# Last layer of a four-layer kernel: each indirect transfer of POOL is sent only after the one in front of it has landed

## The chip, the cores and the metric

One core of a Trainium2 chip runs the whole program. The metric is the device time in microseconds (us) of one execution. The trace is that of one profiled execution, and its times count from the start of its span.

## The reference, cut to what matters

Four layers act on 4096 tokens of 128 features. Each layer normalises x, and adds to it the output of an attention-like block and that of a feed-forward block with experts. The change touches the fourth layer only:

```
xn = _layernorm(x, axis=-1)
x = x + _L3_attn_ref(xn, ...) + _L3_ffn_ref(xn, ...)
return x

def _L3_attn_ref(x, ...):                     # gated attention, 16 batches of 256 tokens in the kernel's tiling
    xn = (x - mu) * rsqrt(var + LN_EPS) * ln_g + ln_b
    uvz = silu(einsum('bld,df->blf', xn, W_in) + b_in)
    u, v, z = (uvz[..., :E], uvz[..., E:2 * E], uvz[..., 2 * E:])
    attn = square(relu(einsum('bqs,bks->bqk', z * gamma_q + beta_q, z * gamma_k + beta_k) / seq_len))
    out = u * einsum('bqk,bke->bqe', attn, v)
    return x + einsum('ble,ed->bld', out, W_out) + b_out

def _L3_ffn_ref(x, wg, w1, b1, w2, b2):       # one expert of 8 for each token, 640 places for each expert
    combine, dispatch = _top1_gate(tokens, wg, capacity)
    dispatched = einsum('sec,sm->ecm', dispatch, tokens)
    h = relu(einsum('ecm,emf->ecf', dispatched, w1) + b1[:, None, :])
    expert_out = einsum('ecf,efm->ecm', h, w2) + b2[:, None, :]
    return einsum('sec,ecm->sm', combine, expert_out)
```

The shapes that are given here are those that the kernel works on: N = 4096 tokens are 32 tiles (NT) of 128 tokens.

## The kernel before

The last layer is `gated_and_experts`. The normalised tokens are in SBUF (`xn_tok`). Routing (L1102 to L1228, on VectorE) works out a place for each token in the buffer `disp`, which lies in HBM: expert e owns the rows from e * 640. It is then signalled with `r_placed` (L1202).

**POOL** has two loops in this layer and nothing else of weight. The scatter (L1598 to L1601) sends 32 indirect transfers, one for each tile: 128 rows of 512 bytes (64 KB) go from `xn_tok` to their places in `disp`. All of them increment the semaphore `scattered`. Then POOL waits until the results of all experts are stored in `ybuf` (semaphores `stored`), and the gather (L1604 to L1608) sends 32 indirect transfers that fetch each token's row from `ybuf` into `gau_gb`, in 8 groups of 4 tiles, each group with its own semaphore `gathered[j]`.

**SP** waits for all 32 transfers of the scatter (L1577, 512 counts), then loads the tokens of experts 0 and 1 (L1568), and later stores results (L1574), loads weights (L1563) and stores the output in 8 pieces, one for each gathered group (L1590).

**TensorE, ScalarE and VectorE** follow a written order of 64 steps, four for each of the 16 batches of the gated attention: scores (L1657), projection (L1631, L1636), values (L1668) and the projection of v (L1648), and the output projection (L1677). Into these steps the 16 chunks of expert work are woven: chunk c belongs to step c + FIRST, FIRST = 23, and its tokens are turned one step earlier, so the first expert work (`turn_tokens`, L1692) stands in step 22, ahead of that step's values. Each engine takes its instructions in this order. The last expert result is taken in step 39, at the end of the tenth batch, and the remaining six batches follow without experts while the gather is under way.

**The combining** of the gathered rows (L1910, on VectorE) is put into the same order: group j stands at this step,

```
return max(Q_GATHER + 3 * (j + 1) + 6, 4 * (GRP * (j + 1) // QT) + 1)
```

with Q_GATHER = 40, that is at steps 49, 52, 55, 58 and 61 for groups 0 to 4, and after step 63 for groups 5 to 7. It waits for 4 transfers of its group (64 counts of `gathered[j]`).

Of the kernel before, what the change touches and what calls it, by code (L numbers as in the profile page):

```python
# [1481 lines left out]
def gated_and_experts(nc, g, t, out, disp, ybuf, r):  # L1482
# [8 lines left out]
    GRP = 4  # L1491
# [4 lines left out]
    with section(nc, "gau", *ROUTE, *names, "w_in", "xs_ready", "turned", "xt_ready",  # L1496
# [44 lines left out]
        gathered = s.sems[len(ROUTE):len(ROUTE) + NGRP]  # L1541
# [15 lines left out]
        with nc.Block() as block:  # L1557

            @block.sync
            def _(sp):  # L1560
                def load_weights(e):
                    sp.wait_ge(s.y_out, 2 * e - 2)
                    sp.dma_start(ew[:, e % 2], t["f3_packed"][e]).then_inc(ew_in[e % 2], 16)  # L1563

                def load_tokens(e):
                    if e >= 2:
                        sp.wait_ge(s.e_turned, 2 * e - 2)
                    sp.dma_start(exin[:, e % 2], disp[e * CAP3:(e + 1) * CAP3, :].rearrange("(t p) d -> p t d", p=P)  # L1568
                                 ).then_inc(ex_in[e % 2], 16)

                def store_result(c):
                    n = CUTS[c % 2][1]
                    sp.wait_ge(s.y_out, c + 1)
                    sp.dma_start(ybuf[chunk_rows(c), :].rearrange("(t p) d -> p t d", p=P),  # L1574
                                 eyo[:, c % 2, 0:n]).then_inc(stored[c % 2], 16)

                sp.wait_ge(s.scattered, NT * 16)  # L1577
                load_tokens(0)
                load_tokens(1)
                for c in range(NC):  # L1580
                    if c % 2 == 1 and c // 2 + 2 < E3:
                        load_tokens(c // 2 + 2)
                    store_result(c)
                    if c % 2 == 1 and c // 2 + 2 < E3:
                        load_weights(c // 2 + 2)
                for j in range(NGRP):
                    sp.wait_ge(s.combined, (j + 1) * GRP)
                    sp.wait_ge(s.f_taken, (j + 1) * GRP // QT)
                    tiles = slice(j * GRP, (j + 1) * GRP)
                    sp.dma_start(out.rearrange("(t p) d -> p t d", p=P)[:, tiles, :],  # L1590
                                 g.x[:, tiles, :]).then_inc(s.out_done, 16)
                sp.wait_ge(s.out_done, NGRP * 16)

            @block.gpsimd
            def _(pool):
                job.gpsimd(pool)
                pool.wait_ge(s.r_placed, 1)
                for i in range(NT):  # L1598
                    pool.indirect_dma_start(disp, bass.IndirectOffsetOnAxis(ap=r.scat_i[:, 0, i:i + 1], axis=0),
                                            g.xn[:, i, :], None, bounds_check=disp.shape[0] - 1,  # L1600
                                            oob_is_err=False).then_inc(s.scattered, 16)  # L1601
                for p in range(2):
                    pool.wait_ge(stored[p], NC // 2 * 16)
                for i in range(NT):  # L1604
                    pool.indirect_dma_start(gb[:, i, :], None, ybuf,  # L1605
                                            bass.IndirectOffsetOnAxis(ap=r.rows_i[:, 0, i:i + 1], axis=0),
                                            bounds_check=ybuf.shape[0] - 1,
                                            oob_is_err=False).then_inc(gathered[i // GRP], 16)  # L1608
# [1413 lines left out]
```

## Time and profile before

| what | us |
| --- | --- |
| median of 3 runs | 1988.49 |
| lowest, highest of them | 1988.32, 2005.57 |
| span of the profiled execution | 2006.6 |
| first transfer of the scatter starts | 1749.01 |
| SP starts to load the tokens | 1791.28 |
| first expert work on TensorE | 1820.85 |
| first transfer of the gather starts | 1926.60 |
| last combining starts | 1999.82 |

No time other than the span is recorded for the profiled execution. The three runs are of other executions of the same program; two of them agree within 0.2 us and the third is near the span. In a timeline row stand the start, the duration, the engine, the line, the operation with what it writes and reads, how many like it were merged, and in brackets how long the engine was idle before it and what the profile infers as having ended that. SP is the engine that issues the plain transfers; POOLq and SPq are the instruction queues of these engines. The busy time of an indirect transfer on POOL is the making of its descriptors; the data moves afterwards.

### The profile page before, as it was taken

Reading aid. Unit: us, or ns where it says so; the run is one execution under the profiler, and the core shown is the slowest. Engines: PE = TensorE matmul, PEld = TensorE weight load, DVE = VectorE, ACT = ScalarE, POOL = GpSimd, SP = SyncE. Lnnn points to the kernel's source line nnn. Section 1 sums busy time; section 2 is a strip of 40 time slices with the busy share of each in tenths; the row PEclk is TensorE's granted clock in tenths of the full one; section 3 lists DMA queues with packets and bytes.
Section 4 is the critical chain, followed back from the end, with each engine's and each line's share of the span. In section 5 each row is a group of like instructions: output and inputs, shape, how many; then the busy total and the mean of one; then the engine's idle time right before and its main releaser. Section 6 shows DMA issues by size and latency. Waiting matters only on the chain. (4 is left out here: it accounts for less than half of the span.)

```text
span 2006.6 us, 34124 instructions
## 1 busy us (share of the span) xinstructions
PE 1593.7 (79%) x12145; PEld 1087.2 (54%) x12146; DVE 1288.1 (64%) x2309; ACT 1058.9 (53%) x1931; POOL 797.6 (40%) x809
## 2 busy tenths in 40 slices
PE   5993788888876776758889998965799999749974
PEld 5661566666654445535567765542344444638863
DVE  7525888788788888764534457758753896724334
ACT  1345787887776764434434444545454777314421
POOL 1447766565669994374212234431400000150041
PEclk9996899999998889658989999987699999569987
DMA  5211011111001110665321124314531341211311
GB/s 151 89 56 44 22 50 56 35 49 50 28 20 35 30 29 23 229 182 88 64 57 59 59 57 81 63 25 131 103 67 42 50 67 17 95 49 51 100 43 55
DMA packets 153335, 130.56 MB, mean 65 GB/s; under 512 B 18929, under 2 KB 137864, under 8 KB 152914
## 3 DMA queue, kind: packets, MB, share of 16 engines
q1 hardware_dynamic: 140554, 104.54, 21.1%
q0 software_dynamic: 12544, 23.82, 4.3%
q8 instruction: 100, 1.64, 0.4%
q14 instruction: 65, 0.53, 0.1%
q10 hardware_dynamic: 72, 0.03, 0.0%
HBM read 77.08 MB, written 52.43 MB: 65 GB/s over the span
## 5 line engine op out<-in xcount | busy, mean ns | idle before, releaser
L746 POOL TENSOR_TENSOR xn_t<-xn_t,scan_du 128x512 f32<-128x512 f32 x256 | 320.9, 1271 | 154.9 <-ACT xn_t L893 105.1
L970 DVE TENSOR_TENSOR_SCAN xn_t<-banks,xn_t 128x512 f32<-128x512 f32 x256 | 311.5, 1217 | 78.7 <-ACT banks L883 42.0
L794 PE MATMUL banks<-scan_hc,ident 128*128 128x256 f32 x1024 | 295.4, 414 | 49.1 <-DVE scan_hc L976 49.1
L2417 ACT ACTIVATE att_pr<-banks 128x768 f32<-128x768 f32 (+1 forms) x256 | 234.3, 917 | 161.9 <-PE banks L2309 76.1
L883 ACT ACTIVATE banks<-delta,scan_exp_centre,a_neg 128x255 f32<-128x255 f32 x512 | 265.0, 559 | 14.8 <-DVE xn_t L970 14.4
L794 PEld LDWEIGHTS banks<-scan_hc,ident 128*128 128x128 f32 x1024 | 193.7, 207 | 110.2 <-DVE scan_hc L976 70.1
L976 DVE TENSOR_TENSOR scan_hc<-xn_t,banks 128x512 f32<-128x512 f32 x256 | 175.8, 687 | 33.4 <-PE banks L779 14.3
L1030 POOL DMA_INDIRECT disp<-xn_tok,places x128 | 135.3, 1057 | 154.6 <-ACT att_pr L2417 44.2
L2325 PE MATMUL banks<-att_pr,att_vx 128*32 128x256 f32 (+1 forms) x2048 | 163.6, 383 | 19.0 <-issue 9.3
L2458 DVE TENSOR_REDUCE att_mb<-banks 128x6 f32<-128x768 f32 x128 | 121.1, 954 | 89.5 <-PE banks L2283 48.7
L2462 DVE TENSOR_REDUCE att_mb<-banks 128x4 f32<-128x1024 f32 x128 | 153.9, 1221 | 18.5 <-PE banks L2276 13.4
L2276 PE MATMUL banks<-att_ks,att_qs 48*128 48x256 bf16 (+1 forms) x1024 | 118.1, 281 | 45.0 <-DMA att_ks<-k_parts 31.2
L893 ACT COPY xn_t<-banks 128x512 f32<-128x512 f32 x128 | 74.5, 582 | 123.7 <-PE banks L770 92.2
L2301 PE MATMUL banks<-att_qs,att_ks 50*128 50x256 bf16 (+1 forms) x1024 | 111.0, 272 | 13.2 <-DMA att_qs<-att_mt 11.0
L1231 POOL IOTA gau_rev<- 128x8 f32 x1 | 0.1, 138 | 302.2 <-POOLq L76 302.2
L1415 POOL DMA_DIRECT2D ybuf<-att_yo x72 | 38.8, 539 | 156.7 <-DVE att_yo L1400 153.1
L1316 PE MATMUL banks<-grouped_w,att_xt 128*128 x288 | 98.4, 465 | 0.5 <-DVE att_xt L1382 0.3
L1605 POOL DMA_INDIRECT gau_gb<-ybuf,rows x32 | 32.2, 1007 | 146.0 <-DMA ybuf<-gau_eyo 136.6
L1365 ACT ACTIVATE att_a<-banks 128x352 f32<-128x352 f32 x72 | 33.4, 463 | 104.8 <-PE banks L1316 104.8
L2276 PEld LDWEIGHTS banks<-att_ks,att_qs 48*128 48x128 bf16 x1024 | 50.1, 101 | 64.2 <-issue 28.5
L779 PE MATMUL banks<-bc,state_sel 96*128 96x256 bf16 x256 | 53.0, 290 | 34.4 <-DVE scan_hc L976 27.7
L2325 PEld LDWEIGHTS banks<-att_pr,att_vx 128*32 128x32 f32 x2048 | 43.5, 110 | 66.0 <-issue 40.7
(384 smaller groups left out, 3339.2 us busy)
## 6 DMA issues: line engine op xcount, KB each, us to landing
scan_ew<-f_packed SPq DMA_DIRECT2D x12, 578.0 KB
q_parts<-att_p_parts SPq DMA_DIRECT2D x16, 384.0 KB, 4.7
k_parts<-att_p_parts SPq DMA_DIRECT2D x16, 384.0 KB, 6.1
att_qs<-q_parts SPq DMA_DIRECT2D x64, 96.0 KB
att_ks<-k_parts SPq DMA_DIRECT2D x64, 96.0 KB
gau_ew<-f_packed SPq DMA_DIRECT2D x8, 578.0 KB
disp<-zeros SPq DMA_DIRECT2D x1, 4608.0 KB, 15.4
att_xin<-disp SPq DMA_DIRECT2D x72, 64.0 KB
```

What stands on the lines that cost most here:

```text
L746: nc.gpsimd.tensor_tensor(bu[:, i % RING], b_sb[:, q % 2], du[:, b % 2, c:c + 1, :].to_broadcast([P, 2, T]), ALU.mult).then_inc(s.bu_made, 1)
L794: ins = nc.tensor.matmul(bank(Y_BANK)[:, c, :], g.ident[:], hc[:, i % RING, n, :], start=False, stop=(i % (PAIRS * DC) == PAIRS * DC - 1 a ...
L883: ins = nc.scalar.activation(bank(DA + i % RING)[:, n, 1:T], delta[:, c, b * T + 1:(b + 1) * T], ACT.Exp, scale=a_neg[:, c, state:state + ...
L970: v.tensor_tensor_scan(rows(h[:, i % 2]), g.ps[:, DA + i % RING, :], rows(bu[:, i % RING]), 0.0, ALU.mult, ALU.add).then_inc(s.scan_done, 1)
L976: v.tensor_tensor(hc[:, i % RING], h[:, i % 2], bank(C_BANK), ALU.mult).then_inc(s.hc_ready, 1)
L1030: pool.indirect_dma_start(disp, bass.IndirectOffsetOnAxis(ap=r.scat_i[:, k, i:i + 1], axis=0), src[:, i, :], None, bounds_check=disp.shape ...
L2276: ins = nc.tensor.matmul(g.ps[:, 2 * m_slot(i) + half, lo:hi], qs[rows_of, p, j, q * P:(q + 1) * P], ks[rows_of, p, j, 0:hi - lo], start=T ...
L2301: ins = nc.tensor.matmul(g.ps[:, 2 * s_slot(i) + half, k * T:k * T + T - q0], ks[rows_of, p, j, k * P:(k + 1) * P], qs[rows_of, p, j, q0:T ...
L2325: ins = nc.tensor.matmul(g.ps[r * 32:(r + 1) * 32, O_BANK, q0:T], vx[:, b % 2, k, 4 * jg + r, :], pr[:, i % RING, half, k * T:k * T + T - q0],
L2417: nc.scalar.activation(pr[:, i % RING], g.ps[:, at:at + 2, 0:W], ACT.Exp, scale=scale).then_inc(s.p_ready, 1)
L2458: v.tensor_reduce(mb[:, b % 2, j, :].rearrange("p (g n) -> p g n", g=2), g.ps[:, at:at + 2, 0:W].rearrange("p g (n k) -> p g n k", k=P), A ...
L2462: v.tensor_reduce(mb[:, b % 2, j, :], g.ps[:, at:at + 2, :].rearrange("p g (n k) -> p (g n) k", k=T), AX_X, ALU.max).then_inc(s.m_taken, 1)
```

## The change

POOL waits ahead of each transfer but the first of each loop until the one in front of it has landed: in the scatter for i * 16 counts of `scattered`, in the gather for the counts of the group that the former transfer belongs to. Nothing else is changed: the same 64 transfers with the same data in the same order.

```
                 for i in range(NT):
+                    if i:
+                        pool.wait_ge(s.scattered, i * 16)
                     pool.indirect_dma_start(disp, bass.IndirectOffsetOnAxis(ap=r.scat_i[:, 0, i:i + 1], axis=0),
                                             g.xn[:, i, :], None, bounds_check=disp.shape[0] - 1,
                                             oob_is_err=False).then_inc(s.scattered, 16)
                 for p in range(2):
                     pool.wait_ge(stored[p], NC // 2 * 16)
                 for i in range(NT):
+                    if i:
+                        pool.wait_ge(gathered[(i - 1) // GRP], ((i - 1) % GRP + 1) * 16)
                     pool.indirect_dma_start(gb[:, i, :], None, ybuf,
                                             bass.IndirectOffsetOnAxis(ap=r.rows_i[:, 0, i:i + 1], axis=0),
                                             bounds_check=ybuf.shape[0] - 1,
```

## Rows read from the trace of the kernel before

**Rows 1.** The scatter's line in all: instructions, durations in ns, first and last start

```profile
L1599 POOLq MOVE  x32: 29/29/29, 1748.2 to 1773.4; - x32
L1599 POOL DMA_INDIRECT disp<-xn_tok,places x32: 977/977/1092, 1749.0 to 1789.1; - x32
```

**Rows 2.** Timeline of POOL, the scatter's first transfer and its last two

```profile
1749.01 1.09 POOL L1599 DMA_INDIRECT disp<-xn_tok,places  x1 [12.82 <-DVEq L1202]
...
1787.78 0.98 POOL L1599 DMA_INDIRECT disp<-xn_tok,places  x1 [0.30 <-issue]
1789.06 0.98 POOL L1599 DMA_INDIRECT disp<-xn_tok,places  x1 [0.30 <-issue]
```

**Rows 3.** Timeline of SP after the scatter, and landing of these loads

```profile
1791.28 0.95 SPq L1568 DMA_DIRECT2D gau_exin<-disp  x2
...
DMA to landing us min/median/max: 3.0/3.3/3.6
```

**Rows 4.** Timeline of TensorE from the scatter's end to the first expert work

```profile
1795.04 2.05 PE L1657 MATMUL banks<-gau_q,gau_k 128*128 128x256 f32 x4 [12.77 <-DVE x_tok L1883]
...
1802.54 1.16 PE L1677 MATMUL banks<-gau_wo,gau_gt 128*128 128x128 f32 x8
...
1804.30 1.10 PE L1657 MATMUL banks<-gau_q,gau_k 128*128 128x256 f32 x4 [0.39 <-DVE x_tok L1883]
...
1809.69 1.16 PE L1677 MATMUL banks<-gau_wo,gau_gt 128*128 128x128 f32 x8
...
1820.85 0.49 PE L1692 MATMUL banks<-ident,gau_exin 128*128 128x128 f32 x3
```

**Rows 5.** Busy time by stretch; the last three columns: TensorE's clock, DMA share, GB/s

```profile
1785.00:1791.00 6.00, 0.00 (x0) 0.00 (x0) 0.69 (x1) 0.63 (x1) 3.91 (x4) 0.50 0.13 46
1795.00:1800.00 5.00, 4.96 (x12) 4.01 (x13) 2.81 (x6) 1.45 (x5) 0.00 (x0) 0.50 0.00 0
1800.00:1810.00 10.00, 9.40 (x46) 7.38 (x45) 5.49 (x12) 3.55 (x9) 0.00 (x0) 0.99 0.00 1
1870.00:1925.00 55.00, 55.00 (x350) 47.48 (x349) 18.70 (x37) 24.24 (x52) 0.00 (x0) 1.00 0.27 80
```

**Rows 6.** The gather's line in all, and its first and last transfer on POOL

```profile
L1605 POOLq MOVE  x32: 29/29/29, 1925.8 to 1951.3; - x32
...
1926.60 1.10 POOL L1605 DMA_INDIRECT gau_gb<-ybuf,rows  x1 [136.56 <-DMA ybuf<-gau_eyo]
...
1967.27 1.00 POOL L1605 DMA_INDIRECT gau_gb<-ybuf,rows  x1 [0.31 <-issue]
```

**Rows 7.** Stretches of 0.05 us around the last data of scatter and gather

```profile
1790.60:1790.65 0.05, 0.00 (x0) 0.00 (x0) 0.00 (x0) 0.00 (x0) 0.00 (x0) 0.50 0.95 339
1790.75:1790.80 0.05, 0.00 (x0) 0.00 (x0) 0.00 (x0) 0.00 (x0) 0.00 (x0) 0.50 0.34 103
...
1969.00:1969.05 0.05, 0.00 (x0) 0.00 (x0) 0.00 (x0) 0.00 (x0) 0.00 (x0) 0.50 1.39 328
...
1969.35:1969.40 0.05, 0.00 (x0) 0.00 (x0) 0.00 (x0) 0.00 (x0) 0.00 (x0) 0.50 0.22 82
```

**Rows 8.** Timeline of VectorE in the gather and at the end, with SP's last stores

```profile
1972.09 0.69 DVE L1877 TENSOR_TENSOR gau_gt<-banks,gau_ut 128x512 f32<-128x512 f32 x1 [14.97 <-DMA k_parts<-att_p_parts]
...
1999.82 3.23 DVE L1910 SCALAR_TENSOR_TENSOR x_tok<-gau_gb,w,x_tok 128x128 f32<-128x128 f32 x12
2000.98 2.47 SPq L1590 DMA_DIRECT2D out<-x_tok  x3
```

**Rows 9.** Layer 1, a gather's transfer that waited for another engine, and its queue

```profile
L2252 POOLq MOVE  x1: 29/29/29, 1191.8 to 1191.8; - x1
...
1192.50 1.00 POOL L2252 DMA_INDIRECT att_gb<-ybuf,rows  x1 [1.53 <-PE banks L2309]
```

**Rows 10.** Layer 0, a scatter's transfer beside a long operation of VectorE

```profile
68.83 4.42 DVE L567 TENSOR_TENSOR x_tok<-x_tok,front_b_out 128x4096 f32<-128x4096 f32 x1
...
70.06 4.05 POOL L1030 DMA_INDIRECT disp<-xn_tok,places  x1 [0.30 <-issue]
```

More of the change, by code:

```diff
@@ L1598, in _ @@
                 for i in range(NT):
+                    if i:
+                        pool.wait_ge(s.scattered, i * 16)
                     pool.indirect_dma_start(disp, bass.IndirectOffsetOnAxis(ap=r.scat_i[:, 0, i:i + 1], axis=0),
@@ L1604, in _ @@
                 for i in range(NT):
+                    if i:
+                        pool.wait_ge(gathered[(i - 1) // GRP], ((i - 1) % GRP + 1) * 16)
                     pool.indirect_dma_start(gb[:, i, :], None, ybuf,
```

## The prediction

> **What bounds the kernel now.** I read the page first, then the timelines of POOL, SP, TensorE and VectorE over the last layer. The last layer has three sections in a row. In the first, POOL sends the scatter while the other engines work on the first batches of the gated attention. The scatter's 32 transfers start 1.28 us apart, from 1749.01 to 1789.06 [rows 1, 2], and SP, which waits for all of them, starts loading tokens at 1791.28 [rows 3]. That load lands about 3.3 us later, at 1794.6, and TensorE uses it at 1820.85 [rows 3, 4]. So **the scatter has 26 us of slack** and is not on the path. What sets 1820.85 is the batches. Undisturbed, one takes 7.15 us (1802.54 to 1809.69), yet TensorE was idle for 12.77 us ahead of 1795.04, for an operation of VectorE [rows 4], and VectorE worked 0.69 of 6 us from 1785 on [rows 5]. The second section, from 1820.85 to the first transfer of the gather at 1926.60, is full: TensorE is busy 55.00 of 55 us [rows 5]. It lasts 105.75 us. In the third, the gather's transfers start from 1926.60 to 1967.27 [rows 6]. Again there is a stop, 14.97 us on VectorE, ended at 1972.09 [rows 8], and the batches set the end; the last 12 combinings run without a pause from 1999.82, when their rows had long landed. So the gather isn't last now either: 1967.27 plus some 2.5 us is 30 us ahead of that.
>
> **What one paced transfer costs.** The change removes nothing, and adds 62 waits on POOL, 31 in each loop. Behind each wait stands only POOL's own next transfer; nothing else is queued there in this layer. Who waits for them is SP (scatter) and VectorE's combining (gather). The period of a paced transfer is a chain of two terms, which the back-to-back loop overlaps.
>
> (a) From the start of a transfer on POOL to the first action of an engine that waits for it. For the scatter one row has it directly: the last one starts at 1789.06 [rows 2] and SP acts at 1791.28 [rows 3], 2.22 us. It isn't delayed by a queue in front of it: its data moves in one burst from 1790.60 to about 1790.80 [rows 7], long after that of the one before (started at 1787.78). For the gather no waiter is visible. Its last transfer starts at 1967.27 [rows 6] and its data moves from 1969.00 to about 1969.35 [rows 7], 2.1 us after the start against 1.75 us in the scatter. With the scatter's 0.45 us from the end of the burst to SP's action this gives 2.55 us. Bounds: 2.1 (nothing after the burst) and 2.8.
>
> (b) From POOL's release to the start of the transfer. Now POOL's queue runs ahead (its last MOVE for the scatter is at 1773.4, the last transfer at 1789.1 [rows 1]), so this is hidden. A queue that stands at a wait can't run ahead. The row where it did stand: MOVE at 1748.2, transfer at 1749.01, 0.8 us [rows 1, 2]; in the gather 1925.8 to 1926.60, 0.8 us [rows 6]; in layer 1 1191.8 to 1192.50, 0.7 us [rows 9]. I take 0.8. Bounds: 0 (if the part after the wait still overlapped) and 0.9, since the transfers after a long pause also took 1.09 instead of 0.98 us [rows 1].
>
> So **the period is 3.02 us in the scatter** (2.22 + 0.8) and **3.35 us in the gather** (2.55 + 0.8), for 1.28 and 1.31 now.
>
> Here a rule of the Trainium skill speaks against so high a price. "DMA: Bandwidth & Descriptors", section "Anatomy of one DMA — SWDGE (gpsimd) path", fits a transfer issued from GpSimd as about 2.0 us plus its bytes over 436e3, which is an estimated 2.15 us for 64 KB. If that were the whole period, both loops would need some 66 us. The trace has nearly this figure for term (a) alone, 2.22 us, and shows 0.8 us outside of it.
>
> **The sum, in the profiled execution.** Scatter: last start 1749.01 + 31 x 3.02 = 1842.6; SP at + 2.22 = 1844.9; tokens + 3.4 = 1848.3. The first expert work moves from 1820.85 to 1848.3, +27.4 us: the 26 us of slack are used up and the path passes to POOL. TensorE is idle for that time, since it finishes the work ahead of step 22 at 1820.85 at the latest. It restarts at the lower of its clock's two levels: after the idle time ahead of 1795 the granted clock was 0.50 (1.2 GHz) until 1800 and 0.99 after [rows 5], and 1795.04 to 1802.54 took 7.50 us where 1804.30 to 1809.69, the same work, took 5.39 [rows 4]. In the full second section that is +2.1 us. Section two starts 27.4 + 2.1 = **29.5 us late**, and its length stays.
>
> Gather: first start 1926.60 + 29.5 = 1956.1; last 1956.1 + 31 x 3.35 = 2059.9; landed for VectorE at + 2.55 = 2062.5. What is late next? The six batches left need 7.15 us each, 43 us, to about 1999, and the combinings at steps 49 to 61 wait for transfers 4 to 20, the last at 1956.1 + 19 x 3.35 + 2.55 = 2022.3. They are through before 2062.5, so only group 7 is left: 4 combinings, 1.1 us (a third of the 3.23 us of the last 12), then the store. Before, the last combining ended at 2003.05 [rows 8] and the span at 2006.6, 3.55 us. The end is 2062.5 + 1.1 + 3.6 = 2067.2, **+60.6 us** against 2006.6: 29.5 from the scatter, 31.1 from the gather.
>
> The span of this execution is 18.1 us above the median of the runs (1988.49), and near the third run (2005.57). I put the difference on the median: 1988.5 + 60.6 = **2049**. If instead the 18 us are stops in sections one and three that the median runs don't have, the paced path, which covers those stops, ends where it ends, and the time is about 2067.
>
> **The rivals.** (1) *The stops are given back and pacing is cheap*: not slower. Mechanism: while POOL sends without a pause, signals from TensorE reach VectorE and ScalarE late: TensorE stood, for an operation of VectorE, until 1795.04 and VectorE until 1972.09, and both went on 5 to 6 us after the last transfer's start [rows 2, 4, 6, 8]. Pacing frees the batches. The gain decides if the tokens land before 1820.85, a period under 2.1 us, and the gather ends before 2006.6, a period under 2.35. With the 2.15 us of that page the times would be 1749.01 + 66.7 + 2.2 + 3.4 = 1821.3, gather from 1929.2, end 1929.2 + 66.7 + 2.5 + 4.7 = 2003.1: -3.5 us, 1985. At a period of 2.0 us the tokens would be there at 1749.01 + 62 + 2.2 + 3.4 = 1816.6, the gather would start at 1926.60 - 4.2 + 2.1 = 1924.5 and the end be 1924.5 + 62 + 2.5 + 4.7 = 1993.7: -13 us, 1976; for 1% faster it would take 1.89. Against it: 2.22 us is measured for (a) alone, with nothing of (b). (2) *The start-up of 0.8 us stays hidden* behind the wait: periods 2.22 and 2.55. Scatter to 1823.4 (+2.6 + 2.1), gather 1931.3 + 79.1 + 2.5 + 4.7 = 2017.6: +11 us, 1999.5. Against it are three rows with 0.7 to 0.8 us. (3) *More than the sum*: transfers take longer. In layer 0 one took 4.05 us beside an operation of 4.42 us on VectorE [rows 10]; those of this layer take at most 0.7 us, but VectorE will be awake more. Each 0.25 us on both periods is +15.5 us; at 3.5 and 3.85 us the end is +90, 2080. The same end comes if signals stay late through the longer scatter, +8 us. "SBUF — State Buffer", section "Who interferes with whom", says that VectorE's 2-port operations lock out GpSimd's descriptors; that the operation of 4.42 us is a tensor_tensor, a kind that the page excludes, is what this trace shows otherwise. (4) *The waits hold nothing up*, because the counts are already there: only possible if a transfer landed within 1.28 us of its start; its data only moves 1.5 us after it [rows 2, 7], which excludes that.
>
> **How the numbers follow.** The forecast (periods within 0.3 us of mine, either reading of the 18 us) has 0.76, from 2049 - 18 = 2031 to 2049 + 18 + 15 = 2082. Rival 3 has 0.12, rival 2 0.07, rival 1 0.04 (of that 0.02 over 1% faster), rival 4 0.01. The range is 2030 to 2082. A measurement of this kernel can tell a change from none at about 1%, 20 us: slower by over 1% takes the forecast and rival 3, and a little of rival 2; rival 2 else and most of rival 1 are within 1%.
>
> **What would show each step.** Right: POOL's transfers of L1599 start 3.0 us apart and those of L1605 3.35, SP's load at 1845, TensorE's L1692 at 1848 after an idle stretch, TensorE full for 106 us afterwards, combinings in groups of 4 some 13 us apart, the last right after the last transfer. Wrong: periods near 2.2, L1692 near 1820, or batches that still stand after the gather's end.

## The result

The changed kernel takes 2065.64 us (median of 4 runs, 2060.17 to 2073.78), the kernel before 1988.4 us (median of 4). The ratio is 1.036, with a 95% interval of 1.030 to 1.042: slower by some 72 us, 77 by the medians. The profiled execution has a span of 2064.5 us.

The page of the changed kernel first. The chain that ended last, which had no part of POOL's transfers in it before, now has them as its first two entries by line:

```profile
span 2064.5 us, 34124 instructions
DMA 8%; PE 5%; issue 2%; DVE 1%; POOLq 0%; ACT 0%; POOL 0%; DVEq 0%
DMA gau_gb<-ybuf,rows 4%; DMA disp<-xn_tok,places 4%; PE banks L1723 2%; PE banks L1710 2%; PE banks L1672 1%; PE banks L1696 0%; PE banks L1652 0%; PE banks L1681 0%; PE banks L1661 0%; PE banks L1640 0%; DMA gau_exin<-disp 0%; DMA ybuf<-gau_eyo 0%; PE banks L1635 0%; PE banks L1626 0%; POOLq L1609 0%
```

The two loops, each line in all (number, durations in ns, first and last start), against [rows 1, 6]:

```profile
L1601 POOL DMA_INDIRECT disp<-xn_tok,places x32: 977/977/1347, 1738.8 to 1833.3; - x32
L1609 POOL DMA_INDIRECT gau_gb<-ybuf,rows x32: 1006/1006/1374, 1947.2 to 2057.2; - x32
```

31 periods take 94.5 us in the scatter, 3.05 us each, and 110.0 us in the gather, 3.55 us each, for 1.29 and 1.31 before. The chain in order of time, around the end of the scatter (start, duration, what), shows the two terms of a period:

```profile
1830.37 2.20 DMA disp<-xn_tok,places
1832.57 0.03 issue
1832.59 0.03 POOLq L1601
1832.62 0.71 issue
1833.33 2.21 DMA disp<-xn_tok,places
1835.54 0.02 issue
1835.56 3.05 DMA gau_exin<-disp
1838.61 0.04 issue
1838.65 0.90 PE banks L1696 x3
```

From the transfer's start on POOL to its landing 2.20 us, then 0.03 us to the MOVE in POOL's queue, and 0.7 us until the transfer starts: 2.96 us here, 3.01 the median. SP acts right behind the last landing, and TensorE 3.1 us later. The same view in the gather, with the landing of 3.23 us the one that falls beside a store of the output, the usual one 2.5 us:

```profile
1976.60 3.23 DMA gau_gb<-ybuf,rows
1979.83 0.02 issue
1979.85 0.03 POOLq L1609
1979.88 0.70 issue
1980.58 2.53 DMA gau_gb<-ybuf,rows
```

TensorE's timeline, against [rows 4]: the batches go on undisturbed beside the paced scatter, 7.15 us each, until the order asks for an expert's tokens:

```profile
1766.96 1.16 PE L1681 MATMUL banks<-gau_wo,gau_gt 128*128 128x128 f32 x8
...
1774.12 1.16 PE L1681 MATMUL banks<-gau_wo,gau_gt 128*128 128x128 f32 x8
...
1838.65 0.90 PE L1696 MATMUL banks<-ident,gau_exin 128*128 128x128 f32 x3 [60.38 <-DMA gau_exin<-disp]
```

So TensorE stands for 60.38 us, not for the 27 that the sum needed. The stops of before (stretches of 5 to 15 us in which an engine stands still for work that has long ended) are gone, and TensorE is ready for the first expert work at 1778.27, 39.5 us after the first transfer, where it took 71.8 us before. Nothing is gained by that here, since the tokens come later still. The busy times by stretch show the restart, against [rows 5] (third column from the right is the clock): 0.50 for the first 5 us and a little more, then full speed.

```profile
1838.60:1843.60 5.00, 4.95 (x13) 4.03 (x14) 1.16 (x2) 0.00 (x0) 0.00 (x0) 0.50 0.06 15
1850.00:1945.00 95.00, 95.00 (x601) 81.85 (x600) 32.87 (x66) 42.43 (x90) 0.00 (x0) 1.00 0.29 85
```

VectorE at the end, against [rows 8]: the combinings (the last three groups here) come in groups of 4, each when its fourth transfer has landed, and the last one 2.7 us after the last transfer's start at 2057.18:

```profile
2032.06 1.14 DVE L1914 SCALAR_TENSOR_TENSOR x_tok<-gau_gb,w,x_tok 128x128 f32<-128x128 f32 x4 [9.66 <-DMA gau_gb<-ybuf,rows]
2045.89 1.14 DVE L1914 SCALAR_TENSOR_TENSOR x_tok<-gau_gb,w,x_tok 128x128 f32<-128x128 f32 x4 [12.69 <-DMA gau_gb<-ybuf,rows]
2059.90 1.14 DVE L1914 SCALAR_TENSOR_TENSOR x_tok<-gau_gb,w,x_tok 128x128 f32<-128x128 f32 x4 [12.87 <-DMA gau_gb<-ybuf,rows]
```

The last layer in three stretches, from the first scatter transfer to the first expert work, from there to the first gather transfer, and from there to the end of the span:

| us | before | after | difference | forecast |
| --- | --- | --- | --- | --- |
| scatter stretch | 71.8 | 99.9 | +28.0 | +27.4 |
| section two | 105.8 | 108.6 | +2.8 | +2.1 |
| gather stretch | 80.0 | 117.3 | +37.3 | +31.1 |
| sum | 257.6 | 325.7 | +68.1 | +60.6 |

The spans differ by 57.9 us only, since the three layers ahead, in which no line differs, took 10.2 us less in this execution (first scatter transfer at 1738.78 for 1749.01).

### The profile page after: what moved, and what is told of

Its sections match the earlier page's. It is cut to its first block and busy times, and to the rows that moved or that the text cites. A ratio compares the mean times of both kernels' runs of the same rounds, so it can differ in the third digit from the quotient of the medians.

```text
span 2064.5 us, 34124 instructions
## 1 busy us (share of the span) xinstructions
PE 1587.4 (77%) x12145; PEld 1087.2 (53%) x12146; DVE 1289.0 (62%) x2309; ACT 1059.6 (51%) x1931; POOL 800.2 (39%) x809
## 5 line engine op out<-in xcount | busy, mean ns | idle before, releaser
L794 PE MATMUL banks<-scan_hc,ident 128*128 128x256 f32 x1024 | 301.3, 421 | 47.1 <-DVE scan_hc L976 47.1
L2329 PE MATMUL banks<-att_pr,att_vx 128*32 128x256 f32 (+1 forms) x2048 | 158.3, 378 | 18.0 <-ACT att_ot L2426 9.3
L1365 ACT ACTIVATE att_a<-banks 128x352 f32<-128x352 f32 x72 | 33.4, 464 | 105.8 <-PE banks L1316 105.8
L2305 PEld LDWEIGHTS banks<-att_qs,att_ks 50*128 50x128 bf16 x1024 | 40.2, 95 | 70.8 <-issue 41.1
```

What stands on the lines that cost most here:

```text
L794: ins = nc.tensor.matmul(bank(Y_BANK)[:, c, :], g.ident[:], hc[:, i % RING, n, :], start=False, stop=(i % (PAIRS * DC) == PAIRS * DC - 1 a ...
L2305: ins = nc.tensor.matmul(g.ps[:, 2 * s_slot(i) + half, k * T:k * T + T - q0], ks[rows_of, p, j, k * P:(k + 1) * P], qs[rows_of, p, j, q0:T ...
L2329: ins = nc.tensor.matmul(g.ps[r * 32:(r + 1) * 32, O_BANK, q0:T], vx[:, b % 2, k, 4 * jg + r, :], pr[:, i % RING, half, k * T:k * T + T - q0],
```

## The experiments

Ratios are to runs of the kernel before on the same chip. The stretches are those of the table.

**Each loop alone.** Only one of the two waits of the change is kept:

```
 scatter_paced: pool.wait_ge(s.scattered, i * 16)                                   # in the scatter, none in the gather
 gather_paced:  pool.wait_ge(gathered[(i - 1) // GRP], ((i - 1) % GRP + 1) * 16)    # in the gather, none in the scatter
```

> Only the scatter's transfers wait for the one in front; the gather is sent as before. Theory (two chains in a row on POOL, each 31 periods long): in the profile of the changed kernel the stretch from the first transfer of the scatter to the first expert work took 99.9 us against 71.8 before, and section two 2.8 us more. So scatter period 3.05 us, +31 us on the profiled execution of before, and 2018 to 2030 us in the runs; the gather keeps its stop of some 15 us on VectorE. Rival (the cost comes from one loop alone, or the two interact): this run lies within 10 us of 1988 or of 2066.

> Only the gather's transfers wait for the one in front; the scatter is sent as before. Theory: from the first transfer of the gather to the end 117.3 us in the changed kernel against 80.0 before, so +37 us, 2025 to 2037 us in the runs, with the scatter's stops still there (first expert work some 72 us after the first scatter transfer) and the gather's gone. The two parts alone add up to the whole, +77 us, within the scatter of the runs. Rival: the gather's pacing is covered by the last six batches, and this run is within 10 us of 1988.

Scatter alone: 2016.05 us, ratio 1.018 (1.013 to 1.023), +35 us by the ratio and +36 by the medians. Stretches 99.9, 108.6 and 76.7 us. Gather alone: 2014.18 us, ratio 1.020 (1.012 to 1.027), +39 us by the ratio and +34 by the medians. Stretches 68.8, 105.7 and 113.1 us. Both times lie below the forecasts in us, but this chip ran the kernel before at 1980 us, and the forecasts were for 1988: against that they were +30 to +42 and +37 to +49. The parts add up to +70 (medians) or +74 (ratios), the whole to +72 to +77: two chains one behind the other. Each ratio is known to some 10 to 15 us only, so a small interaction isn't excluded; by the stretches of one execution each, the parts give +27.6 and +30.1, and the whole +68.1; the missing 10 us lie in the two stretches that were left as they were (3.1 and 3.3 us shorter than before) and in the gather (113.1 for 117.3). Apart from that the stretches of the loop that was left as it was are those of before, stops included: VectorE's timeline of the run with the paced scatter shows one in its gather,

```profile
1979.12 0.69 DVE L1879 TENSOR_TENSOR gau_gt<-banks,gau_ut 128x512 f32<-128x512 f32 x1 [16.56 <-DMA k_parts<-att_p_parts]
```

and of these two runs only the one with the paced scatter has the 2.8 us in section two (108.6 for 105.7).

**What the long periods of the gather are.** The changed kernel with one line more on SP, ahead of the stores of the output:

```
+                sp.wait_ge(s.combined, NT)
                 for j in range(NGRP):
                     sp.wait_ge(s.combined, (j + 1) * GRP)
```

> The changed kernel with the 8 stores of the output held back until all tokens are combined. Theory (each store of the output collides with the transfer that is then under way and makes it land 0.6 us later; 7 of the 31 periods of the gather are such): the periods of 3.8 us disappear, the mean falls from 3.55 to 3.4 us, and the stretch from the gather's first transfer to its last shrinks by 4 us; the end then pays for 2 MB of stores, some 8 us. Rival (the long periods come with the group's semaphore or the combining on VectorE, not the store): they stay.

```profile
L1610 POOL DMA_INDIRECT gau_gb<-ybuf,rows x32: 1006/1006/1112, 1936.7 to 2040.7; - x32
```

The mean period is now 104.0 / 31 = 3.35 us, for 3.55, so the 31 periods are 6.0 us shorter in all. The stores are 3.9 us of that: the seven periods in which a store is sent add up to 27.4 us in the changed kernel and 23.5 here, which is what was expected. Another 1.8 us is one period of 5.04 us that is 3.23 here, and has no store in it (it is the one that met a load of instructions, see below). The gather stretch is level (117.8 for 117.3 us), since the stores are paid for at the end instead. One execution, 2056.24 us; its first three layers took 10.5 us less than those of the changed kernel's profile, so the time itself tells nothing, the stretches do.

**Why the kernel before had stops at all.** They made the pacing look cheaper than it is, and the prediction left them without a cause. Six kernels bear on the candidates: the number of transfers under way, POOL's queue running ahead, POOL being busy, and descriptors made back to back. Two of them wait for the transfer two or three places in front, with that many semaphores in turn (`sent`, `fetched`), for which SP and the combining wait as well:

```
+                    if i >= DS:                                  # DS = 2 or 3
+                        pool.wait_ge(sent[i % DS], i // DS * 16)
                     pool.indirect_dma_start(disp, ...).then_inc(sent[i % DS], 16)
```

> Each transfer waits for the one two places in front (two semaphores in turn), so up to two are under way. Theory: the period halves to 1.53 us in the scatter and 1.77 us in the gather, just above POOL's own 1.28 and 1.31, with a pause of 0.2 to 0.5 us on POOL. If the late signals of the kernel before come from POOL's queue running ahead of its transfers (theory Q), the stops are gone: scatter stretch 53 us for 72, gather stretch 62 for 80, and the time is 1955 to 1972 us, faster than before. If they come from POOL being busy with descriptors nearly all the time (theory B), the stops mostly stay, and the time is 1985 to 2010 us.

> Each transfer waits for the one three places in front. The landing chain allows a period of 1.0 us, so POOL works back to back at its own 1.28 us, as before, but its queue can't run more than three transfers ahead. Theory Q (queue running ahead makes signals late): stops gone, first expert work some 47 us after the first scatter transfer, time 1945 to 1965 us. Theory B (POOL busy back to back makes signals late): the stops stay as in the kernel before, time within 10 us of 1988.

Depth 2: 1959.74 us, ratio 0.989 (0.984 to 0.994). Periods 1.61 and 1.76 us, stretches 55.4, 108.0 and 62.0 us: the stops are gone, and it is faster than the kernel before. That is what theory Q had forecast, and not what theory B had (1985 to 2010 us): a pause at every second transfer is enough, since the scatter's periods mostly alternate between 1.30 and 1.71 us. Depth 3: 1975.31 us, ratio 0.997 (0.994 to 1.001), no difference that can be told from none, where theory Q had 1945 to 1965 us. Periods 1.29 and 1.34, stretches 67.6, 105.7 and 75.4 us. Its scatter shows what a stop is; the timeline of all engines:

```profile
1746.96 2.08 PE L1686 MATMUL banks<-gau_wo,gau_gt 128*128 128x128 f32 x8 [4.95 <-DVE gau_gt L1886]
...
1748.83 0.63 PE L1631 MATMUL banks<-ident,gau_xs 128*128 128x128 f32 x2
...
1749.06 0.69 DVE L1878 TENSOR_TENSOR gau_vb<-banks,gau_bv 128x512 f32<-128x512 f32 x1 [2.16 <-remote]
1749.79 0.63 ACT L1802 ACTIVATE gau_v<-gau_vb 128x512 f32<-128x512 f32 x1 [6.96 <-DVE gau_vb L1878]
...
1763.03 0.42 DVE L1892 TENSOR_TENSOR x_tok<-x_tok,banks 128x256 f32<-128x256 f32 x1 [13.28 <-DMA att_ks<-k_parts]
...
1763.60 2.04 PE L1666 MATMUL banks<-gau_q,gau_k 128*128 128x256 f32 x4 [14.14 <-issue]
...
1768.63 0.56 ACT L1778 ACTIVATE gau_xt<-banks,gau_ln_b,gau_ln_g 128x256 f32<-128x256 f32 x1 [18.22 <-DMA front_b_out<-m_b_out]
```

VectorE's L1892 waits for the matmuls of L1686, which ended at 1749.04 and whose banks it adds, and starts at 1763.03, 14 us late. ScalarE's L1778 waits for signals of TensorE alone, the last of them that of L1631, which ended at 1749.46, and starts at 1768.63, 19 us late. (The profile names loads of other layers as releasers, which can't be.) VectorE's own signals come at once: ScalarE takes one after 0.04 us (1749.75 to 1749.79), TensorE one after 0.15 us (1763.45 to 1763.60). Late are the signals that TensorE gives, as far as the profile can tell, which models the ends of matmuls. So depth 3 speaks against the queue: it hardly runs ahead there (its last MOVE is at 1766.4, the last transfer of the scatter at 1768.0, 16 us apart before), and the stops are nearly as before.

**A pause without a landing.** Nothing waits for a transfer; POOL clears some columns of a spare tile ahead of each one (8 tiles in turn, whose wait is met long before):

```
+                    nc.gpsimd.memset(spare[:, i % 8, :], 0.0).then_inc(s.spaced, 1)    # 512, 256 or 128 columns
                     pool.indirect_dma_start(...)
```

> Nothing waits for a landing. Ahead of each of the 64 transfers POOL clears 512 columns of a spare tile, 0.5 us, so transfers start some 1.8 us apart with POOL's queue free to run ahead. Theory B (signals come late while POOL makes descriptors back to back; a pause of descriptors is enough): the stops are gone, first expert work 31 x 1.8 + 5.4 = 61 us after the first scatter transfer, gather to the end 31 x 1.8 + 7.4 = 63 us, and the time is 0.5 to 1.3% below before. Rival (it is the wait for a landing that clears the stops): stops as before, time up to 15 us above before.

> As the run with the spacer, but 128 columns, 0.2 us, so a period of some 1.5 us. Theory B with a small pause being enough: scatter stretch 52 us, gather to the end 55 us, 1.5 to 2% below before, the fastest of all. If the pause has to be longer than 0.5 us (with 0.3 us already between two transfers): stops in part, time between before and 1% below.

> 256 columns, period some 1.5 us. If the residual stops of the 128-column run (5 + 4 + 4 us in its scatter) are gone at this pause, the scatter stretch is 31 x 1.5 + 5.5 = 52 us, the gather to the end 54 us, and the time is level with the run of 128 columns, 2.0 to 2.6% below before. If they only shrink with the pause in proportion, the scatter stretch is over 53 us.

| columns | us | ratio (interval) | periods | stretches |
| --- | --- | --- | --- | --- |
| 512 | 1954.69 | 0.983 (0.979 to 0.988) | 1.74, 1.75 | 59.2, 107.8, 61.5 |
| 256 | 1941.08 | 0.978 (0.973 to 0.982) | 1.52, 1.53 | 52.6, 108.4, 54.7 |
| 128 | 1941.31 | 0.977 (0.972 to 0.981) | 1.40, 1.46 | 53.7, 105.6, 52.6 |

POOL's timeline at 256 columns, for the size of the pause:

```profile
1746.41 0.98 POOL L1603 DMA_INDIRECT disp<-xn_tok,places  x1 [0.17 <-issue]
1747.38 0.34 POOL L1602 MEMSET gau_spare<- 128x256 f32 x1
1747.88 0.97 POOL L1603 DMA_INDIRECT disp<-xn_tok,places  x1 [0.17 <-issue]
```

A pause of 0.50 us between two descriptor phases, for 0.30 before, lets the batches run at 7.15 us, though POOL's queue runs 9 us ahead of its transfers there (last MOVE 1759.7, last transfer 1769.1); at 128 columns, 0.40 us, TensorE still stood 4.91 us in one place:

```profile
1768.47 2.05 PE L1664 MATMUL banks<-gau_q,gau_k 128*128 128x256 f32 x4 [4.91 <-DVE x_tok L1890]
```

512 columns did better than expected (1.7% below for 0.5 to 1.3). The expectation of 128 columns (1.5 to 2% below) was passed a little (2.3%), and its own alternative holds in part too: the stops shrink with the pause, and are small enough at 0.40 us. The two shorter pauses give the fastest versions, 2.2 and 2.3% below the kernel before, and they wait for no landing at all. At 256 and 512 columns TensorE again stands for the tokens ahead of the first expert work (13.0 and 20.6 us), so there a shorter period would still gain.

**A busy POOL.** The changed kernel, with 3 x 512 columns cleared behind each transfer:

> The changed kernel, every transfer still waiting for the one in front, but POOL clears three times 512 columns (1.5 us) behind each transfer, in the time in which it would wait. Rival P (signals are late because POOL is busy, with whatever): the stops come back in the scatter, the batches no longer take 7.15 us each. Theory B (the descriptors do it): batches undisturbed, periods stay near 3.05 and 3.5 us, time as the changed kernel, 2060 to 2075 us.

```profile
1742.34 0.97 POOL L1602 DMA_INDIRECT disp<-xn_tok,places  x1 [0.56 <-issue]
1743.32 1.47 POOL L1608 MEMSET gau_spare<- 128x512 f32 x3
1745.34 0.97 POOL L1602 DMA_INDIRECT disp<-xn_tok,places  x1 [0.56 <-issue]
...
1749.70 1.16 PE L1690 MATMUL banks<-gau_wo,gau_gt 128*128 128x128 f32 x8
1756.86 1.16 PE L1690 MATMUL banks<-gau_wo,gau_gt 128*128 128x128 f32 x8
1764.01 1.16 PE L1690 MATMUL banks<-gau_wo,gau_gt 128*128 128x128 f32 x8
```

POOL is busy 2.44 of 3.0 us, and the batches take 7.15 us (one later takes 8.2), stretches 100.8, 107.6 and 117.4 us, 2063.79 us in one run. It isn't POOL's being busy, it is the indirect transfers close behind each other. Whether that is the making of their descriptors or the moving of their data isn't separated, since both are equally dense in every one of these kernels; nor is the length of the pause separated from the share of time that descriptors take (0.98 of 1.28 us with stops, of 1.37 us with small ones, of 1.47 us with none). The clearing adds little to a period (mean 3.08 and 3.51 us, for 3.05 and 3.55): it hides behind the landing.

## Why the prediction was right

**The period.** Term (a) was forecast as 2.22 us from one row and is 2.20 to 2.27 in 28 of the scatter's 32 transfers, 2.37 to 2.95 in the others. In the gather 2.55 was forecast, and it is 2.5 to 2.7 us where nothing collides, with 2.81 and 2.94 as exceptions. Term (b), 0.8 us, is 0.76 us with the MOVE. The scatter's period is 3.01 us (median; mean 3.05) for 3.02 forecast, the gather's 3.35 (median) for 3.35. The reading of SP's start as the landing of the last transfer, and of the MOVE as the time of release, held.

**The scatter.** The slack of 26 us was used up and no more was hidden: +28.0 us for +27.4. Four late landings lengthened the mean period to 3.05 us; the tokens needed 3.1 us for 3.4. The first expert work came 99.9 us after the first transfer; 1848.3 - 1749.0 = 99.3 had been forecast.

**The restart at the low clock.** +2.8 us for +2.1. The granted clock was 0.50 until 1844.1 and 0.70 in the stretch from there to 1845.0, which makes some 6.0 us at half speed, all full of matmuls: 3.0 us lost (an estimate). For the batch of the prediction the same count gives 0.50 until 1800.0 and 0.71 to 1800.5, 5.2 us at half speed, also full. And the batch at full speed with which it was compared had 0.22 us of waiting for VectorE ahead of its L1668, which the slow one didn't have, so that part of the slow clock's cost was hidden there.

**The gather: a term that was sized too small.** "Last 1956.1 + 31 x 3.35" took the collision-free period for all 31. The mean is 3.55: seven transfers of the gather meet a store of the output (256 KB), which the order of the kernel sends just when a group of 4 is complete, and land after 3.05 to 3.32 us, 0.5 to 0.8 us later than usual, some 4.2 us in all; one shares its time with a load of instructions and lands after 4.28 us, 1.7 us late; the rest is the two exceptions. 31 x 0.2 = 6.2 us, all of the miss in this stretch. Without the collisions the forecast period holds: the experiment with the late stores measures 3.35. (The run with the gather alone has 3.41 with its stores, so single executions differ by some 0.1 us in this.) The prediction had named neither collision.

**The base.** 2049 puts the +60.6 on the median of the runs. With the measured stretches it would have been 1988.5 + 68.1 = 2056.6, and 2065.6 came. So of the 16.6 us between forecast and result the sum's terms explain 7.5. The other reading in the prediction, 2067, was near the number for a wrong reason: it took the 18 us between the profile of before and the median for longer stops in the last layer. In two executions of kernels that have the same scatter or gather, that stretch was only 3.1 and 3.3 us shorter. The three layers ahead, which are the same in all these kernels, varied much more: their end, the first scatter transfer, lies between 1720.9 and 1740.0 us in the ten other profiles, and at 1749.0 in that of before. The remaining 9 us between 2056.6 and the median are within that variation and were not located.

**The rivals.** Of (1) the mechanism was there, the price wasn't: the stops vanish in every kernel with pauses of 0.5 us or more, and the depth-2 run shows that landing pacing at half the period is a gain of 1.1%. At a period of 3 us the batches' gain only lengthens TensorE's wait. (2), the hidden 0.8 us, and (4) are excluded by the chain's rows. (3), transfers held up by VectorE, didn't show in this layer: the median duration on POOL is 977 ns as before and the longest 1374 ns, with VectorE at work. The long transfer of layer 0 is there in the changed kernel too (4.04 us). The Trainium skill's fit of about 2.0 us plus the bytes over 436e3 for such a transfer ("DMA: Bandwidth & Descriptors", section "Anatomy of one DMA — SWDGE (gpsimd) path") gives an estimated 2.15 us; the 2.20 us of the scatter from POOL's start to the landing agree, the 2.5 to 2.7 us of the gather lie above. It isn't the period of a chain of them, which has 0.76 us more.

## What to carry to other kernels

A wait for a landing turns a pipeline into a chain: cost it as (start to landing) + (release to start), both readable in the trace before the change, times the number of links, and subtract only the slack of whoever waits for the last link. Then ask which other transfers the new, later places of the links will meet; here that was the largest term missed. And ask whether the work that seems to bound the kernel is really held up by the loop that has slack: a loop of indirect transfers that was 26 us early slowed the work beside it by 32 us (71.8 for 39.5), and sending it a little less densely, by a pause of 0.5 us, was worth 2.2%.

## What the runs showed of the hardware that was not expected

While POOL sends indirect transfers with only 0.3 us between the descriptors of two of them, signals from TensorE to VectorE and ScalarE come late, by 14 and 19 us in the rows of depth 3, while the signals from VectorE to ScalarE and TensorE in the same rows come within 0.15 us. It doesn't depend on a queue that runs ahead (it hardly does at depth 3, with stops, and runs 9 us ahead at 256 columns, without), nor on POOL's being busy (81% of a period in the run with the busy POOL, and 90% at 256 columns, both without stops). The amount of traffic doesn't suffice either: the DMA share in the scatter of before is some 0.14, and section two runs full at 0.27 [rows 5]. It shrinks at a pause of 0.4 us and isn't seen at 0.5 us, nor at depth 2, where every second pause is longer. The trace has no record of a signal's way, so what holds them up stays open.

The section "Instruction fetch mechanics" of the Trainium skill's page "Runtime: NRT & Kernel Launch" says that the loading of instructions is mostly hidden. That such loads aren't the cause of the stops fits with it: two fall into the scatter of before, fewer than its stops, and four into the paced scatter, which has none. In a chain of landings a load isn't always hidden. One moved 1.8 us after the start of a transfer of the paced gather, which landed after 4.28 us instead of 2.5; the same pair in the run with the busy POOL landed after 3.95 us, and a pair in the paced scatter after 2.95 instead of 2.24. A load that moved between two transfers left the next landing as it was (2.25 us in the paced scatter), and so did one that moved 2.25 us after a start (2.47 us, late stores). That the load makes the landing late is read from these coincidences, and wasn't tested.
